# Layer-norm statistics kept as 128x128 blocks in four column groups, and the mixer's last output parts taken half by half

## The reference

```python
x = x + _L0_attn_ref(_layernorm(x, axis=-1), ...)   # state-space mixer, 8192 inner features
x = x + _L0_ffn_ref(_layernorm(x, axis=-1), ...)    # picks one row of every 32 by argmax
x = x + _L1_attn_ref(_layernorm(x, axis=-1), ...)   # attention with 32 heads
x = x + _L1_ffn_ref(_layernorm(x, axis=-1), ...)    # dense layer behind a selection
```

```python
var = jnp.mean(jnp.square(y), axis=-1, keepdims=True)
y = y * jax.lax.rsqrt(var + EPS) * norm_w
y = y * jax.nn.silu(gate)
return y @ out_proj_w.T
```

## Time and profile before

| | us |
|---|---|
| median of 3 runs | 2432.32 (2431.52 to 2433.32) |
| the profiled execution, as timed | 2436.1 |
| its span, first to last instruction | 2434.3 |
| TensorE busy | 2236.8 (92%) |
| VectorE busy | 1642.8 (67%) |
| ScalarE busy | 1175.1 (48%) |
| GpSimd busy | 686.7 (28%) |

### The profile page before, as it was taken

One profiled execution on the slowest core, in us unless ns is written; L12 is line 12 of the kernel. 1 busy time (PEld: TensorE's weight loads), 2 busy tenths in 40 slices (PEclk: granted clock), 3 DMA queues, 4 the chain that ended last, 5 costly groups with the idle time before them and its releaser, 6 DMA issues.

```text
span 2434.3 us, 34263 instructions
## 1 busy us (share of the span) xinstructions
PE 2236.8 (92%) x13940; PEld 1740.2 (71%) x13940; DVE 1642.8 (67%) x1707; ACT 1175.1 (48%) x1747; POOL 686.7 (28%) x318
## 2 busy tenths in 40 slices
PE   4589999999999999999999999994799889999987
PEld 2478877777777777787887777773378657777754
DVE  5667767777777776777776777675822347777754
ACT  2244545445545554454454545451533247777741
POOL 1023343334333333343334333422344200000000
PEclk8789999999999999999999999997999989999998
DMA  1111011101011010111101110100122110000000
GB/s 66 47 37 37 28 45 37 36 28 54 28 37 37 29 51 30 37 38 44 37 28 44 38 36 28 45 19 4 31 80 95 59 27 16 21 22 22 10 24 35
DMA packets 41627, 89.31 MB, mean 37 GB/s; under 512 B 13824, under 2 KB 22912, under 8 KB 41088
## 3 DMA queue, kind: packets, MB, share of 16 engines
q1 hardware_dynamic: 41472, 87.12, 11.5%
HBM read 83.82 MB, written 3.28 MB: 36 GB/s over the span
## 4 chain that ended last, share of the span: by engine, by line
PE 67%; DVE 15%; ACT 5%; issue 4%; DMA 4%; POOL 3%; SPq 0%; ACTq 0%; DVEq 0%
PE PS L472 15%; PE PS L473 14%; PE PS L474 14%; DVE arena L1220 5%; DMA arena<-in_w_xg 4%; PE PS L703 3%; PE PS L550 3%; PE PS L788 3%; POOL wol L393 2%; PE PS L773 2%; PE PS L466 2%; DVE arena L1250 1%; ACT arena L907 1%; PE PS L795 1%; PE PS L762 1%
## 5 line engine op out<-in xcount | busy, mean ns | idle before, releaser
L472 PE MATMUL PS<-xnh,wh 128*128 128x512 f32 x1272 | 512.4, 403 | 23.4 <-DVE xnl L1160 10.9
L474 PE MATMUL PS<-xnh,wl 128*128 128x512 f32 x1272 | 499.3, 393 | 0.0
L473 PE MATMUL PS<-xnl,wh 128*128 128x512 f32 x1272 | 498.9, 392 | 0.0
L1220 DVE SCALAR_TENSOR_TENSOR arena<-PS,arena 128x1020 f32<-128x1020 f32 (+2 forms) x240 | 305.5, 1273 | 93.1 <-ACT arena L920 47.3
L385 POOL TENSOR_TENSOR arena<-arena 128x1024 f32<-128x1024 f32 x64 | 173.2, 2706 | 464.4 <-ACT arena L899 464.4
L472 PEld LDWEIGHTS PS<-xnh,wh 128*128 128x128 f32 x1272 | 240.4, 189 | 83.4 <-issue 20.7
L474 PEld LDWEIGHTS PS<-xnh,wl 128*128 128x128 f32 x1272 | 240.4, 189 | 51.1
L473 PEld LDWEIGHTS PS<-xnl,wh 128*128 128x128 f32 x1272 | 240.7, 189 | 46.5
L380 POOL TENSOR_TENSOR wl<-arena,wh 128x1024 fp32r<-128x1024 f32 x72 | 172.6, 2397 | 301.2 <-ACT wh L882 301.2
L887 ACT ACTIVATE PS<-PS 128x1024 f32<-128x1024 f32 x128 | 129.2, 1009 | 264.9 <-PE PS L519 264.9
L472 PE MATMUL PS<-zh,woh 128*128 128x512 f32 x512 | 215.0, 420 | 26.2 <-DVE arena L1220 16.9
(11 more groups left out here) (221 smaller groups left out, 4274.5 us busy)
## 6 DMA issues: line engine op xcount, KB each, us to landing
arena<-in_w_xg SPq DMA_DIRECT2D x72, 512.0 KB, 3.7
arena<-in_w_o SPq DMA_DIRECT2D x32, 512.0 KB, 3.6
arena<-in_w_f SPq DMA_DIRECT2D x28, 512.0 KB, 3.5
arena<-in_w_h SPq DMA_DIRECT2D x16, 257.0 KB
arena<-scr SPq DMA_DIRECT2D x256, 6.0 KB
x<-in_x SPq DMA_DIRECT2D x1, 2048.0 KB, 7.6
arena<-scr SPq DMA_DIRECT2D x128, 3.0 KB
out<-x SPq DMA_DIRECT2D x1, 2048.0 KB, 6.3
```

Source lines behind the costliest of these rows:

```text
L472: mm(PS[:, bank], ah, bh, start=(n == 0), stop=False)
L473: mm(PS[:, bank], ah, bl, start=False, stop=False)
L474: last = mm(PS[:, bank], al, bh, start=False, stop=(n == len(terms) - 1))
L1220: ins = stt(o, pair_of(bank).rearrange("p q (b t) -> p q b t", t=SEQ)[:, :, :, :SEQ - k], w[:, 3 - k:4 - k], o, ALU.mult, ALU.add)
```

## The change

**Statistics.** `narrow` makes a sum over partitions with 32 weight columns instead of 128, on a quarter of the tokens of the half at a time: chunk `c` of 128 tokens goes to partitions 32c to 32c+31, a column group of its own, so the 512 sums of a half stand in one 128x128 block (the same number in all 32 partitions of a group). ScalarE copies the mean to SBUF; root and reciprocal are taken on 128x128. `widen` then spreads a row again: one matmul for each group, with one partition of the block as moving operand and one partition of a constant of ones as weights, into four banks. VectorE's subtraction and product read their second operand from these four banks (`wide_row`). `onesI` becomes `ones`, which VectorE sets to 1.0 at the start. A root of one element stands ahead of each norm on ScalarE. On TensorE the mean of half 0 waits for half 0 alone; on VectorE both reciprocals stand ahead of both products. Norm 2's projections go to other banks.

**End of the mixer.** VectorE makes the last `zl` (L1377 of the new file), and GpSimd only the last squares. TensorE sums `sumsq` ahead of the output parts. The eight output parts are taken one half at a time, half 0 first, in four banks; the factor's root and reciprocal (128x256) are taken under the first two, and spread into banks 4 to 7 behind the second. VectorE adds a part to `sq` and multiplies it, GpSimd adds it to `x`. `layernorm(1)` begins with half 0 when its four parts are in, and SyncE's wait for `x1` goes (the clearing by GpSimd, for which it waits also, stands behind the additions).

```diff
...
-        identF, causal, onesD, onesI = (cst[:, n * P:(n + 1) * P] for n in range(4))
+        identF, causal, onesD, ones = (cst[:, n * P:(n + 1) * P] for n in range(4))
...
+        def chunk(h, c):
+            return slice(h * HALF + c * P, h * HALF + (c + 1) * P)
...
+        def in_chunks(v):
+            return v.rearrange("p k (c t) -> p k c t", t=P)
...
+        def wide_row(first, at):
...
+            return PS[:, first:first + 4, at:at + P].unsqueeze(1).to_broadcast([P, KD, 4, P])
...
-            sp.wait_ge(s["x1"], 1)
...
-            z_low(NT - 1, 1)
...
-            po.wait_ge(s["x1"], 1)
...
+            for n in range(2 * KD):
+                h, m = divmod(n, KD)
+                po.wait_ge(s["ol_m"], n + 1)
+                nc.gpsimd.tensor_tensor(x[:, m, half(h)], x[:, m, half(h)], sq[:, m, half(h)], ALU.add).then_inc(s["x1"], 1)
...
-            def layernorm(n):
-                for h in range(2):
-                    for k in range(KD):
-                        last = mm(PS[:, A + h], onesD, x[:, k, half(h)], start=(k == 0), stop=(k == KD - 1))
-                    last.then_inc(s["ln_mean"], 1)
+            def narrow(bank, at, ones_of, v, h):
...
+                for k in range(v.shape[1]):
+                    for c in range(4):
+                        last = mm(PS[32 * c:32 * c + 32, bank, at:at + P], ones_of[:, 0:32], v[:, k, chunk(h, c)],
+                                  start=(k == 0), stop=(k == v.shape[1] - 1))
+                return last
...
+            def widen(first, at, v):
+                for c in range(4):
+                    R = slice(32 * c, 32 * c + 1)
+                    last = mm(PS[:, first + c, at:at + P], ones[R], v[R], start=True, stop=True)
+                return last
...
+            def layernorm(n, ready, clear=None, sd=sdn):
+                def mean(h):
+                    for name, count in ready[h]:
+                        pe.wait_ge(s[name], count)
+                    narrow(4 * h, P, onesD, x, h).then_inc(s["ln_mean"], 1)
...
+                def mean_wide(h):
+                    pe.wait_ge(s["ln_m"], 2 * n + h + 1)
+                    widen(4 * h, 0, sd[:, col(h)]).then_inc(s["ln_mw"], 1)
...
+                mean(0)
+                if clear:
+                    pe.wait_ge(s[clear[0]], clear[1])
+                    mean_wide(0)
+                    mean(1)
+                else:
+                    mean(1)
+                    mean_wide(0)
+                mean_wide(1)
...
-                    for k in range(KD):
-                        last = mm(PS[:, C + h], onesD, sq[:, k, half(h)], start=(k == 0), stop=(k == KD - 1))
-                    last.then_inc(s["ln_var"], 1)
+                    narrow(4 * h, P, onesD, sq, h).then_inc(s["ln_var"], 1)
+                for h in range(2):
+                    pe.wait_ge(s["ln_rc"], 2 * n + h + 1)
+                    widen(4 * h, 0, sd[:, col(2 + h)]).then_inc(s["ln_rw"], 1)
...
+            pe.wait_ge(s["ssq"], NT + 1)
+            for h in range(2):
+                last = narrow(LB, col(2 + h).start, ones, sumsq.unsqueeze(1), h)
+            last.then_inc(s["f0_ps"], 1)
...
-            pe.wait_ge(s["zlo"], NT + 1)
-            for m in range(KD):
-                pe.wait_ge(s["oacc"], 2 * (NT - 2) - 1 + m)
-                out_part(m, GB if m % 2 else XB)
...
-            pe.wait_ge(s["ssq"], NT + 1)
-            pe.wait_ge(s["oacc"], 2 * NT)
-            for h in range(2):
-                mm(PS[:, A + h], onesI, sumsq[:, half(h)], start=True, stop=True).then_inc(s["f0_ps"], 1)
...
-            pe.wait_ge(s["x1"], 1)
-            layernorm(1)
+            pe.wait_ge(s["zlo"], NT)
+            pe.wait_ge(s["zlast"], 1)
+            for n in range(2 * KD):
+                h, m = divmod(n, KD)
+                if n < KD:
+                    pe.wait_ge(s["oacc"], 2 * (NT - 2) - (n < 2))
+                else:
+                    pe.wait_ge(s["ol_x"], n - KD + 1)
+                split(XB + n % KD, [(woh[:, kk, col(m)], wol[:, kk, col(m)], zh[:, kk, half(h)], zl[:, kk, half(h)])
+                                    for kk in range(2)]).then_inc(s["ol_ps"], 1)
+                if n == 1:
+                    pe.wait_ge(s["f0_rc"], 1)
+                    for hh in range(2):
+                        last = widen(LB, hh * P, sd[:, col(hh)])
+                    last.then_inc(s["f0_w"], 1)
...
+            layernorm(1, ([("x1", KD), ("ol_x", KD + 1)], [("x1", 2 * KD)]), clear=("ol_x", 2 * KD))
...
-            pe.wait_ge(s["x2"], 2)
-            layernorm(2)
+            layernorm(2, ([("x2", 1)], [("x2", 2)]))
...
-            layernorm(3)
+            layernorm(3, ([], []))
...
+                act(sd[:, HALF:HALF + 1], epsc, ACT.Sqrt)
+                for h in range(2):
+                    ac.wait_ge(s["ln_mean"], 2 * n + h + 1)
+                    act(sd[:, col(h)], PS[:, 4 * h, P:2 * P], ACT.Copy).then_inc(s["ln_m"], 1)
...
-                    act(sd[:, half(h)], PS[:, C + h], ACT.Sqrt, bias=epsc).then_inc(s["ln_sd"], 1)
+                    act(sd[:, col(2 + h)], PS[:, 4 * h, P:2 * P], ACT.Sqrt, bias=epsc).then_inc(s["ln_sd"], 1)
...
-            for h in range(2):
-                ac.wait_ge(s["f0_ps"], h + 1)
-                act(sd[:, half(h)], PS[:, A + h], ACT.Sqrt, bias=epsc).then_inc(s["f0_sd"], 1)
+            ac.wait_ge(s["f0_ps"], 1)
+            act(sd[:, 0:2 * P], PS[:, LB, 2 * P:4 * P], ACT.Sqrt, bias=epsc, scale=1.0 / INTER0).then_inc(s["f0_sd"], 1)
...
-                    ve.wait_ge(s["ln_mean"], 2 * n + h + 1)
-                    tt(xn[:, :, half(h)], x[:, :, half(h)], across(PS[:, A + h].unsqueeze(1), (P, KD, HALF)),
-                       ALU.subtract).then_inc(s["ln_xc"], 1)
+                    ve.wait_ge(s["ln_mw"], 2 * n + h + 1)
+                    tt(in_chunks(xn[:, :, half(h)]), in_chunks(x[:, :, half(h)]), wide_row(4 * h, 0), ALU.subtract)\
+                        .then_inc(s["ln_xc"], 1)
...
-                    link(V.reciprocal(sd[:, half(h)], sd[:, half(h)]))
-                    tt(xn[:, :, half(h)], xn[:, :, half(h)], across(sd[:, half(h)].unsqueeze(1), (P, KD, HALF)),
-                       ALU.mult).then_inc(s["ln_xn"], 1)
+                    V.reciprocal(sd[:, col(2 + h)], sd[:, col(2 + h)]).then_inc(s["ln_rc"], 1)
+                for h in range(2):
+                    ve.wait_ge(s["ln_rw"], 2 * n + h + 1)
+                    tt(in_chunks(xn[:, :, half(h)]), in_chunks(xn[:, :, half(h)]), wide_row(4 * h, 0), ALU.mult)\
+                        .then_inc(s["ln_xn"], 1)
...
+            V.memset(ones, 1.0).then_inc(s["ones"], 1)
...
-            for m in range(KD):
-                out_sum(m, GB if m % 2 else XB, 2 * (NT - 2) + 1 + m)
-            ve.wait_ge(s["oacc"], 2 * NT)
-            for h in range(2):
-                ve.wait_ge(s["f0_sd"], h + 1)
-                link(V.reciprocal(sd[:, half(h)], sd[:, half(h)]))
-            link(tt(sq[:, :, :], sq[:, :, :], across(sd[:, :].unsqueeze(1), (P, KD, TOK)), ALU.mult))
-            tt(x[:, :, :], x[:, :, :], sq[:, :, :], ALU.add).then_inc(s["x1"], 1)
-            ve.wait_ge(s["x1"], 1)
+            ve.wait_ge(s["zhi"], NT)
+            tt(zl[:, 1], zt[:, 1], zh[:, 1].bitcast(F32), ALU.subtract).then_inc(s["zlast"], 1)
+            ve.wait_ge(s["oacc"], 2 * (NT - 2))
+            ve.wait_ge(s["f0_sd"], 1)
+            V.reciprocal(sd[:, 0:2 * P], sd[:, 0:2 * P]).then_inc(s["f0_rc"], 1)
+            for n in range(2 * KD):
+                h, m = divmod(n, KD)
+                o = sq[:, m, half(h)]
+                ve.wait_ge(s["ol_ps"], n + 1)
+                tt(o, o, PS[:, XB + n % KD], ALU.add).then_inc(s["ol_x"], 1)
+                if n == 0:
+                    ve.wait_ge(s["f0_w"], 1)
+                ve.wait_ge(s["ol_x"], n + 1)
+                o = o.rearrange("p (c t) -> p c t", t=P)
+                tt(o, o, PS[:, LB:LB + 4, col(h)], ALU.mult).then_inc(s["ol_m"], 1)
...
```

More of the change, by code:

```diff
@@ L482, in _ @@
             pe.wait_ge(s["first_in"], 16 * 5)
-            layernorm(0)
+            pe.wait_ge(s["ones"], 1)
+            layernorm(0, ([], []), sd=sd)
             pe.wait_ge(s["dt_w"], 2)
```

16 lines of the change are left out of this document (8 added, 8 removed).

## The result

The changed kernel takes 2394.3 us (median of 4 runs, 2391.07 to 2395.55) against 2432.82 for the kernel before in the same measurement: ratio 0.984, 95% interval 0.9823 to 0.9857, so 38.5 saved. The forecast was 2391.1, with 41.2 saved. Its profiled execution took 2393.2, with a span of 2391.4.

A forecast was written before the change was run, and what follows sets the result against it. TensorE held 67% of the chain of waits, except in the norms and mixer's end, where engines take turns. Savings of 23.2, 10.5, 3.6 and 3.9 sum to 41.2, from median 2432.32 to 2391.1 us; 8-in-10 range 2381 to 2409.

The forecast's parts named there:

- mixer's end and norm 1: Last output parts through norm 1: first projection done at 1706.0 instead of 1729.2, saving 23.2 us.
- norm 0: First layer norm: TensorE goes on at 32.5 instead of 43.07, saving 10.5 us.
- norm 2 with the cold entry: Norm before attention: 6.2 us shorter, less 2.6 for projections entered at half clock; saving 3.6.
- norm 3 with the cold entry: Norm before the last layer: 5.1 us shorter, less 1.2 for short passes entered cold; saving 3.9.
- what the change doesn't touch: Stages outside the four norms and the mixer's end: no saving forecast, 0.
- Price of `narrow`: Sums over partitions: four column groups side by side, 0.87 us at full clock and 1.7 at half.
- Other prices: Norms and mixer's end: reciprocals 0.95 (128 columns) and 1.75 (256), root 0.25, GpSimd add 1.25, VectorE part 1.44 us.
- Cold entries: Work behind norms 2 and 3: TensorE starts at half clock, costing 2.6 and 1.2 us.
- A: `narrow` in norms and mixer's end: only two column groups overlap; saving 24.5, total 2408 us; chance 0.2.
- B: Norms 1 to 3: clock stays high, so cold entries and halved `narrow` come back; 2385 us; chance 0.13.
- C: `narrow`: four groups run one after another, 6.8 us each at half clock; 2446 us, slower; chance 0.04.
- D: Behind the last residual part: small weights `c2` and `c1` land late, price 0 to 3; 2393 us; chance 0.08.

The follow-up runs named there:

- first pair: First traces of the unchanged kernel before and of the changed kernel; their profiled executions took 2436.1 and 2393.2 us.
- second pair: Second traces of the same two kernels, both rerun unchanged; medians 2434.07 us for the kernel before and 2395.43 us for the changed kernel.
- the two experiments on the order: Changed kernel with `narrow` reordered: one column group after another, 2404.36 us; two groups at a time, 2396.39 us.
- fill_123: Changed kernel plus idle TensorE matmuls, results unused, in the pauses inside norms 1, 2 and 3; 2392.59 us, ratio 0.9834.
- fill_all: fill_123 plus idle matmuls in norm 0: 20 while input loads, 5 inside, 6 before the mixer's first matmul; 2384.75 us, ratio 0.9801.
- groups_serial: Changed kernel with `narrow` finishing all feature tiles of one column group before the next; 2404.36 us, ratio 0.9875.
- end_only: Changed kernel's new end of the mixer, with the wide layer-norm statistics of the kernel before; 2413.12 us, ratio 0.9913.
- fill_tuned: fill_all with fewer idle matmuls behind norm 0 and before norm 2's first variance, one more between norm 2's means; 2389.2 us, ratio 0.9823.
- before 2: Second trace of the kernel before, rerun unchanged; median 2434.07 us, ratio 1.0004, profiled execution 2435.09 us.
- after 2: Second trace of the changed kernel, rerun unchanged; median 2395.43 us, ratio 0.9847 to the kernel before.

## Why the prediction was right, and where it was off

Point by point, each term against the two pairs of traces:

| term | forecast | first pair | second pair |
|---|---|---|---|
| mixer's end and norm 1 | -23.2 | -24.4 | -24.4 |
| norm 0 | -10.5 | -10.4 | -8.2 |
| norm 2 with the cold entry | -3.6 | -4.0 | -3.9 |
| norm 3 with the cold entry | -3.9 | -3.7 | -3.6 |
| what the change doesn't touch | 0 | -0.4 | +0.7 |
| sum | -41.2 | -42.9 | -39.4 |

- **Price of `narrow`.** 0.87 and 1.7 were forecast, 26 and 49 ns a pass are 0.83 and 1.57: four groups do run side by side. This held the forecast together, and the two experiments on the order show how it would have failed.
- **Other prices.** Reciprocals 0.95 for 128 columns and 1.75 for 256, the table loads out of the norms, GpSimd's additions 1.29 each, VectorE's part 1.32 instead of 1.44, the spreading of 16 passes 0.73: all near what was taken. The root of 128 took 0.37 and not 0.25. Two readings were off without harm: the two column groups of the earlier trace rows began a pass every 0.055, not 0.052 (at 1658.37 the last four of the 48 begin), and the 2.79 of L1306 was not slow work beside L385 but a wait for the operation of GpSimd before it (last section).
- **Mixer's end and norm 1** gave 1.2 more than forecast, from errors that partly cancel. The parts were 2.2 faster: the clock was up after six passes, at 1659.3, where twelve at half clock were forecast, so VectorE began its first product 4.9 behind the first matmul and not 6.2; and a part took it 1.32. The norm behind them was 1.2 slower: half 1's mean with its hand-overs took 3.21 instead of 2.55 and the variance 1.94 instead of 1.55, both at half clock throughout (the wait for GpSimd's last addition, 1.4, was as forecast), and the root 0.37. The hand-over was 0.4 slower and the first projection 0.6 faster.
- **Norm 0** began at 11.83 and 11.42 and not at 11.0: the loads came later, and 0.2 of it is the new wait for `ones`, which VectorE sets first. It ended at 32.64 and 31.97 all the same, where 32.5 was forecast.
- **Cold entries.** 2.6 and 1.2 were forecast, 2.3 to 2.4 and 0.9 to 1.1 came. That it is the clock is shown by the windows above, 0.52 behind norm 2. Behind norm 3 the price is so small because before, too, the clock fell after 1 us; the forecast had read full clock from norm 3's own passes alone. The idle matmuls took 0.6 of the one and 0.2 of the other back.
- **Rivals.** A (two groups at a time) is refuted by the 26 ns, and even its order of issue costs only some 3, since groups still overlap at the turn: its 2408 was too high. B did not come, and was too high a price: `fill_123`, which does in norms 1 to 3 most of what B supposed, gives 3.6 in the stages where B had 5.8. That `fill_all` has 2384.7, near B's 2385, is chance, since it gains in the preparation and the tiles. C did not come either; group after group, in `groups_serial`, makes 2404 and not 2446, with 4.08 for a `narrow` at half clock where C has 6.8. D did not come: the last of the eight loads was issued by 1679.35 (the first row below), which with the 4.5 of the earlier trace rows is 1683.9 at the latest, and the projection at 1686.08 was released by VectorE's product. Timeline of after, SyncE and GpSimd:

```profile
1676.67 2.68 SPq L344 DMA_DIRECT2D arena<-in_c  x4
...
1680.76 1.68 POOL L434 CAST zl<-arena 128x1792 fp32r<-128x1792 f32 x1 [5.88 <-DMA arena<-in_c]
```


**What was mis-sized** is the last step, from the stages to the median. The four terms held: the changed places gave 42.5 in the first pair of traces and 40.1 in the second, against the 41.2 of the forecast. The medians gave 38.5 and 36.5. The profiled execution of before was 3.8 above the median (that of after 1.1 below its own), and I let the whole saving stand while taking those 3.8 to lie outside it. Part of them can lie in norm 0, whose 43.07 holds more half clock than the 40.16 of the second trace; against that one the change gives 8.2 and not 10.5. But 43.07 is no rare value: `end_only`, with the old norm code, has 42.79. The five traces with the new norm 0 and no idle matmuls in it have 31.97 to 32.64, so norm 0 is worth 9.8 on average, 7.5 to 11 from trace to trace. The rest of the gap is not placed. The mixer stretch alone, with the same code, runs from 1613.88 to 1619.84 over the ten traces without idle matmuls ahead of it, which is more than the gap. That the total came within 3 of the median is therefore in part luck; that it came out near the stages is not.

**What makes one execution longer.** In the mixer stretch the traces' clock shows most of it. Between its 64 tiles spells of half clock, nearly all of 3.4 us, stand 8 to 10 times, at other tiles in each trace. Windows of after, ahead of, in and behind one of them:

```profile
700.00:706.90 6.90, 4.88 (x28) 3.60 (x27) 6.20 (x6) 4.82 (x6) 1.96 (x1) 1.00 0.01 3
706.90:710.30 3.40, 3.40 (x10) 2.66 (x9) 2.47 (x3) 0.67 (x1) 0.00 (x0) 0.50 0.53 157
710.30:717.00 6.70, 6.70 (x73) 5.51 (x72) 3.39 (x3) 0.94 (x1) 0.00 (x0) 1.00 0.01 2
```

| trace | mixer stretch | of it at half clock |
|---|---|---|
| fill_all | 1612.32 | 88.7 |
| before | 1615.74 | 93.4 |
| after | 1616.47 | 94.0 |
| fill_tuned | 1617.10 | 92.2 |
| before 2 | 1618.97 | 97.2 |
| after 2 | 1619.03 | 97.1 |

About 60 of each sum lie in the preparation, the first tiles and just before the last tile, the same in every trace within a few us. Over all twelve traces the two go together (correlation 0.93, 0.66 us of stretch for 1 us at half clock). That a spell lengthens the stretch is plain from the passes in it, which begin 0.43 apart instead of 0.23. What decides where a spell falls was not tried.

## What to carry to other kernels

A reduction over partitions on a narrow result is better written as four column groups taken in turn, the group innermost in the loop: here 1.08 for the sums of a half and 0.50 for the spreading against some 3.6 at full clock, and a reciprocal and root on a fourth of the columns. Price it at both clock levels and charge the stage behind it, because here TensorE, with less to do in the norms, came out of norm 2 at half clock. Before a saving of 1 or 2% is read off one trace, take a second trace of the kernel before: a stage of 40 us differed by 2.9 between two executions.

## What was not expected of the hardware

- The order of issue alone sets the overlap of column groups: 26 ns from pass to pass with four groups in turn, 41 in pairs, 71 group after group, all for 128 columns of 32-bit floats at full clock.
- Two engines on operands in SBUF took turns. VectorE's L1306 takes 1.28 alone and 2.79 at the last tile, where it started while GpSimd's L393 ran until 1661.83: 1.71 of waiting and 1.08 of work. All 31 times in before that L1306 started beside an operation of GpSimd, it took the rest of that operation and 1.08 more, within 0.01; so did the `zl` of after (0.95 and 1.08). It goes both ways: GpSimd's squares take 2.35 at 1643.87 and 3.33 beside the rest of L1306, with or without VectorE's `zl` behind it (3.32 and 3.33). VectorE's L1302, with an operand in PSUM, took its 1.28 beside GpSimd's L389 and L393. Timeline of before:

```profile
1641.78 1.28 DVE L1306 SCALAR_TENSOR_TENSOR arena<-arena 128x1024 f32<-128x1024 f32 x1
...
1643.87 2.35 POOL L385 TENSOR_TENSOR arena<-arena 128x1024 f32<-128x1024 f32 x1 [16.30 <-ACT arena L899]
...
1659.48 2.35 POOL L393 TENSOR_TENSOR wol<-arena,woh 128x1024 fp32r<-128x1024 f32 x1
```

- Matmuls whose output nobody reads save time where TensorE waits anyway: with 20 of them ahead of norm 0 its two means take 1.95 instead of 3.64.
- A fill of the wrong length costs what it gave: in `fill_all` the six behind norm 0's product held the preparation until 32.41; with three it started at 31.30.
